# Setting the attention stage's constants at the start and loading its first two heads during the first stage of a fused transformer layer

## The reference

```python
xn  = layernorm(x)                                   # over the last axis
qkv = einsum('bld,ed->ble', xn, w_qkv); q, k, v = split(qkv, 3); q, k = rope(q), rope(k)
att = softmax(einsum('blhd,bmhd->bhlm', q, k) / sqrt(16))
a   = einsum('bhlm,bmhd->blhd', att, v) @ w_out.T
h   = silu(xn @ (w_gate/127).T) * (xn @ (w_up/127).T)    # integer weights
out = x + a + h @ (w_down/127).T
```

## Time and profile before

| | |
|---|---|
| median of 3 runs | 3239.01 us (3239.01 to 3239.97) |
| the profiled execution | 3237.97 us, its span 3236.2 us |
| mean granted TensorE clock | 0.972 of full speed |
| busy: PE, DVE, ACT, POOL | 92%, 87%, 75%, 13% of the span |
| stage A's last store issued | 544.21 us |
| first matmul of stage B | 576.85 us |

### The profile page before, as it was taken

The page is one execution under the profiler, slowest core; times in us unless marked ns, Lnnn a source line. Parts: engine busy times, 40 slices in busy tenths (PEclk is TensorE's granted clock), DMA queues, the critical chain, the costliest instruction groups (busy, mean ns, idle before and its releaser), DMA issues.

```text
span 3236.2 us, 65472 instructions
## 1 busy us (share of the span) xinstructions
PE 2986.2 (92%) x19736; PEld 915.1 (28%) x19736; DVE 2807.7 (87%) x3214; ACT 2413.1 (75%) x4609; POOL 435.8 (13%) x672
## 2 busy tenths in 40 slices
PE   5888886699999999999999999999999999999999
PEld 3555553122222222222222222222222222222225
DVE  6666764899999999999999999999999999999972
ACT  4445353288888888888888888888888888888883
POOL 2545445000000000000000000000000000000000
PEclk9999998699999999999999999999999999999999
DMA  2222222011111111111111011111111111111125
GB/s 92 78 96 76 88 84 63 26 28 29 29 28 29 28 29 28 29 28 29 28 29 30 27 31 27 32 26 31 28 30 28 30 28 30 28 30 28 30 61 163
DMA packets 124612, 137.04 MB, mean 42 GB/s; under 512 B 43264, under 2 KB 103296, under 8 KB 124288
## 3 DMA queue, kind: packets, MB, share of 16 engines
q1 hardware_dynamic: 124288, 132.79, 15.0%
HBM read 88.15 MB, written 34.08 MB: 38 GB/s over the span
## 4 chain that ended last, share of the span: by engine, by line
PE 77%; DVE 7%; issue 7%; POOL 3%; ACT 3%; DMA 1%; DVEq 0%; SPq 0%; ACTq 0%; POOLq 0%
PE psum L679 31%; PE psum L695 29%; PE psum L644 14%; DVE row_max L1196 2%; PE psum L627 2%; ACT probs L805 1%; POOL qk_rot L834 1%; POOL parts L840 1%; PE psum L554 1%; PE psum L577 1%; POOL hT L846 1%; ACT silu L749 1%; DVE xn L977 1%; DVE y_blk L1117 1%; DVE rot_s L1095 0%
## 5 line engine op out<-in xcount | busy, mean ns | idle before, releaser
L1196 DVE TENSOR_REDUCE row_max<-psum 128x1 f32<-128x1024 f32 x2048 | 2402.7, 1218 | 166.0 <-PE psum L644 142.9
L805 ACT ACTIVATE probs<-psum 128x512 f32<-128x512 f32 x4096 | 2130.6, 602 | 407.9 <-PE psum L695 405.0
L695 PE MATMUL psum<-q_op,k_op 51*128 51x512 f16 x4096 | 1249.7, 387 | 42.2 <-ACT probs L805 20.2
L644 PE MATMUL psum<-k_op,q_op 48*128 48x512 f16 x4096 | 1047.0, 393 | 97.1 <-issue 43.8
L679 PE MATMUL psum<-probs,v_op 128*32 128x512 f32 x8192 | 1104.6, 611 | 8.3
L695 PEld LDWEIGHTS psum<-q_op,k_op 51*128 51x128 f16 x4096 | 314.5, 94 | 1359.0 <-ACT probs L805 1235.3
L915 POOL TENSOR_TENSOR acc_sb<-acc_sb,inv_rows 128x512 f32<-128x512 f32 x64 | 81.6, 1276 | 1841.4 <-DMA inv_rows<-inv_dram 1841.4
L644 PEld LDWEIGHTS psum<-k_op,q_op 48*128 48x128 f16 x4096 | 217.5, 94 | 389.9 <-DVE row_max L1196 302.5
L679 PEld LDWEIGHTS psum<-probs,v_op 128*32 128x32 f32 x8192 | 163.3, 108 | 262.3 <-issue 244.1
L742 ACT ACTIVATE parts<-qk_rot 128x512 f16<-128x512 f32 x64 | 40.3, 630 | 244.1 <-POOL qk_rot L834 244.1
L554 PE MATMUL psum<-xnT,w 128*128 128x512 f16 x768 | 184.6, 388 | 9.9 <-DVE h L1108 9.9
(11 more groups left out here) (102 smaller groups left out, 1019.1 us busy)
## 6 DMA issues: line engine op xcount, KB each, us to landing
qk_dram<-staged SPq DMA_DIRECT2D x64, 256.0 KB, 2.9
q_op<-qk_dram SPq DMA_DIRECT2D x128, 128.0 KB
k_op<-qk_dram SPq DMA_DIRECT2D x128, 128.0 KB
x_ln<-in_x SPq DMA_DIRECT2D x16, 512.0 KB, 3.5
x_res<-in_x SPq DMA_DIRECT2D x16, 512.0 KB, 4.2
y_dram<-y_blk SPq DMA_DIRECT2D x16, 512.0 KB, 3.1
k_op<-qk_dram SPq DMA_DIRECT2D x128, 64.0 KB
q_op<-qk_dram SPq DMA_DIRECT2D x128, 64.0 KB
```

The lines of the kernel that those rows point to most:

```text
L644: mm = pe.matmul(bank(2 * half + j), q_op[r:r + ROWS, s, t * P:(t + 1) * P], k_op[r:r + ROWS, s, cols:cols + BANK], start=True, stop=True)
L695: pe.matmul(bank(b), k_op[r:e, h % SLOTS, t * P:(t + 1) * P], q_op[r:e, h % SLOTS, j * BANK:(j + 1) * BANK], start=True, stop=True).then_i ...
L805: nc.scalar.activation(probs[:, g2 % 2, j * BANK:(j + 1) * BANK], bank(b), ACT.Exp, scale=to_score).then_inc(s2_used, 1)
L1196: nc.vector.tensor_reduce(row_max[:, hl % 2, t, half:half + 1], psum[:, 2 * half * BANK:(2 * half + 2) * BANK], AX.X, ALU.max).then_inc(s1 ...
```

## The change

The eleven tensors get SBUF of their own (they are allocated with `keep`, before stage A's buffers, instead of over them). To make room `qk_rot` goes from four buffers to two, so `qk_sum(k, t)` now waits for `lo_part` of two tiles before instead of four. Six of the seven constants move to the start of GpSimd's list, around the cast of the down weights; the constant in `k_op` is written as pairs in 32-bit words. `inv_rows`, which still overlaps stage A's buffers, is cleared where it was, with a semaphore of its own (`rows_cleared`). `load_head(0)` and `load_head(1)`, 16 DMAs, move from after stage A to the point between SP's blocks 13 and 14; they wait for the stores of blocks 0 to 3, which hold the first sequence.

```diff
+STAB_ONE_PAIR = struct.unpack("<f", struct.pack("<ee", STAB_ONE, STAB_ONE))[0]
...
+    q_op = sb(keep, "q_op", [P, SLOTS, TILES * P], F16)
+    k_op = sb(keep, "k_op", [P, SLOTS, TILES * P], F16)
+    v_op = sb(keep, "v_op", [P, 2, TILES, 32])
...
-    qk_rot = sb(sa, "qk_rot", [P, BLK, 2 * D])
+    qk_rot = sb(sa, "qk_rot", [P, 2, 2 * D])
...
         with sp.Fori(1, NBLK - 2) as k:
             block_a(k, 2)
+        sp.wait_ge(b_const, 2)
+        sp.wait_ge(staged_out, 16 * N_STAGED * (TILES // BLK))
+        load_head(0, 0)
+        load_head(1, 0)
         block_a(NBLK - 2, 1)
         block_a(NBLK - 1, 0)
...
-        sp.wait_ge(b_const, 2)
-        load_head(0, 0)
-        load_head(1, 0)
-        sp.wait_ge(b_const, 7)
+        sp.wait_ge(rows_cleared, 1)
...
-        pe.wait_ge(b_const, 7)
+        pe.wait_ge(b_const, 6)
...
         nc.gpsimd.tensor_copy(identh[:, :], ident[:, :]).then_inc(identh_ready, 1)
+        k_words = k_op[:, :, :].rearrange("p s n -> p (s n)").bitcast(F32)
+        pool.wait_ge(identh_ready, 1)
+        nc.gpsimd.memset(k_words[32:HALF, :], STAB_ONE_PAIR).then_inc(b_const, 1)
+        pool.wait_ge(b_const, 1)
+        nc.gpsimd.memset(k_words[HALF + 32:P, :], STAB_ONE_PAIR).then_inc(b_const, 1)
         pool.wait_ge(wdown_loaded, 16)
+        pool.wait_ge(b_const, 2)
         nc.gpsimd.tensor_copy(nat["d"], nat["di"]).then_inc(down_float, 1)
+        pool.wait_ge(down_float, 1)
+        nc.gpsimd.memset(v_op[:, :, :, DH:32], 1.0).then_inc(b_const, 1)
+        ... (stab, zero and unit in the same way, each waiting for the one before)
+        pool.wait_ge(b_const, 6)
         pool.wait_ge(prep, MAT_MAX_READY)
...
-            if not (isinstance(k, int) and k == 0):
-                pool.wait_ge(parts_ready, BLK * (k - 1) + t + 1)
-            nc.gpsimd.tensor_tensor(qk_rot[:, t, :], rot_c[:, t % 2, :], rot_s[:, t % 2, :],
+            if t >= 2 or not (isinstance(k, int) and k == 0):
+                pool.wait_ge(parts_ready, BLK * k + t - 1)
+            nc.gpsimd.tensor_tensor(qk_rot[:, t % 2, :], rot_c[:, t % 2, :], rot_s[:, t % 2, :],
...
-        nc.gpsimd.memset(k_op[32:HALF, :, :], STAB_ONE).then_inc(b_const, 1)
-        ... (all seven constants)
+        nc.gpsimd.memset(inv_rows[:, :], 0.0).then_inc(rows_cleared, 1)
```

More of the change, by code:

```diff
@@ L14 @@
+import struct
 from contextlib import ExitStack
@@ L110, in layer_program @@
     exp_scale = sb(keep, "exp_scale", [P, 2])
+    q_op = sb(keep, "q_op", [P, SLOTS, TILES * P], F16)
+    k_op = sb(keep, "k_op", [P, SLOTS, TILES * P], F16)
+    v_op = sb(keep, "v_op", [P, 2, TILES, 32])
+    row_max = sb(keep, "row_max", [P, 2, TILES, 2])
+    neg_max = sb(keep, "neg_max", [P, TILES])
+    neg_rem = sb(keep, "neg_rem", [P, TILES])
+    neg_unit = sb(keep, "neg_unit", [P, TILES])
+    zero = sb(keep, "zero", [P, TILES])
+    unit = sb(keep, "unit", [P, TILES])
+    stab = sb(keep, "stab", [P, P // TILES, TILES], F16)
+    stabT = sb(keep, "stabT", [STAB_PARTS * TILES, P], F16)
     sa = ExitStack()
@@ L180, in layer_program @@
     sB = ExitStack()
-    q_op = sb(sB, "q_op", [P, SLOTS, TILES * P], F16)
-    k_op = sb(sB, "k_op", [P, SLOTS, TILES * P], F16)
     probs = sb(sB, "probs", [P, 2, TILES * P])
[L184 to L192, removed]
     acc_sb = sb(sB, "acc_sb", [P, 2, BANK])
@@ L258, in layer_program @@
     b_const = sem("b_const")
+    rows_cleared = sem("rows_cleared")
     qk_loaded = [sem(f"qk_loaded{s}") for s in range(SLOTS)]
@@ L385, in block_a @@
                 sp.dma_start(x_res[:, :, :], x_blocks[k + 1]).then_inc(xres_loaded, 16)
[L387 to L398, removed]
         def load_head(hl, i):
@@ L410, in load_head @@
                 sp.dma_start(k_op[r + DH:r + 3 * DH, s, :], src[1, 0:2]).then_inc(qk_loaded[s], 16)
+        sp.dma_start(x_res[:, :, :], x_blocks[0]).then_inc(xres_loaded, 16)
+        load_x(1)
+        block_a(0, 2)
+        with sp.Fori(1, NBLK - 2) as k:
+            block_a(k, 2)
+        sp.wait_ge(b_const, 2)
+        sp.wait_ge(staged_out, 16 * N_STAGED * (TILES // BLK))
+        load_head(0, 0)
+        load_head(1, 0)
+        block_a(NBLK - 2, 1)
+        block_a(NBLK - 1, 0)
+        sp.wait_ge(staged_out, 16 * N_STAGED * NBLK)
+        sp.wait_ge(y_out, 16 * NBLK)
+        sp.wait_ge(down_full, BLK * NBLK)
         def load_stab(hl, i):
@@ L741, in hi_part @@
                 act.wait_ge(partsT_full, BLK * k)
-            nc.scalar.activation(parts[:, t, 0, :], qk_rot[:, t, :], ACT.Copy).then_inc(part_hi, 1)
+            nc.scalar.activation(parts[:, t, 0, :], qk_rot[:, t % 2, :], ACT.Copy).then_inc(part_hi, 1)
         def block_a(k, last):
@@ L815, in _ @@
         nc.gpsimd.tensor_copy(identh[:, :], ident[:, :]).then_inc(identh_ready, 1)
+        k_words = k_op[:, :, :].rearrange("p s n -> p (s n)").bitcast(F32)
[3 more added lines that the diff above has]
+        nc.gpsimd.memset(k_words[HALF + 32:P, :], STAB_ONE_PAIR).then_inc(b_const, 1)
         pool.wait_ge(wdown_loaded, 16)
+        pool.wait_ge(b_const, 2)
         nc.gpsimd.tensor_copy(nat["d"], nat["di"]).then_inc(down_float, 1)
+        pool.wait_ge(down_float, 1)
+        nc.gpsimd.memset(v_op[:, :, :, DH:32], 1.0).then_inc(b_const, 1)
+        pool.wait_ge(b_const, 3)
+        nc.gpsimd.memset(stab[:, :, :], 0.0).then_inc(b_const, 1)
+        pool.wait_ge(b_const, 4)
+        nc.gpsimd.memset(zero[:, :], 0.0).then_inc(b_const, 1)
+        pool.wait_ge(b_const, 5)
+        nc.gpsimd.memset(unit[:, :], 1.0 / STAB_ONE).then_inc(b_const, 1)
+        pool.wait_ge(b_const, 6)
         pool.wait_ge(prep, MAT_MAX_READY)
@@ L839, in lo_part @@
             pool.wait_ge(part_hi, BLK * k + t + 1)
-            nc.gpsimd.tensor_tensor(parts[:, t, 1, :], qk_rot[:, t, :], parts[:, t, 0, :],
+            nc.gpsimd.tensor_tensor(parts[:, t, 1, :], qk_rot[:, t % 2, :], parts[:, t, 0, :],
                                     ALU.subtract).then_inc(parts_ready, 1)
@@ L1164, in _ @@
         block_a(NBLK - 1, 0)
-        dve.wait_ge(b_const, 7)
+        dve.wait_ge(b_const, 6)
         def add_y(half):
```

## The result

| | before | after |
|---|---|---|
| median | 3239.01 us | 3218.45 us (3216.76 to 3218.58, 4 runs) |
| ratio | | 0.9936, 95% interval 0.9919 to 0.9953 |
| profiled execution: own time, span | 3237.97, 3236.2 | 3218.38, 3216.6 |
| last store of stage A issued | 544.21 | 555.09 |
| first row maximum of stage B begins | 577.57 | 556.53 |

The change makes the kernel faster by 20.6 us, clearly more than 0.2%, but by less than the 27.0 us forecast, and 3218.45 lies outside the range of 3207 to 3217. The table says where to look: the gap between the stages went as forecast, but stage A ends 10.9 us later instead of 4.7, and stage B takes 1.5 us more. In stage A three things add up: it starts late, its blocks are longer by the new waits, and TensorE's clock falls to half in more of its blocks.

What follows compares the result with a forecast made beforehand. Bound: the chain from stage A's last store through fills and loads to stage B's first matmul, with TensorE, VectorE and ScalarE idle. −31.65 + 3.5 + 1.2 = −27.0 us, span 3209.2, median 3212.0 us, range 3207 to 3217.

Steps and rivals of the forecast that it cites:

- the growth of stage A: Stage A was to end 4.7 us later, from added GpSimd waits (3.5) and small fills at the start (1.2).
- The gap: Between stages A and B: fills and loads no longer delay the first matmul, only the branch out of the If; −31.65 us.
- The sixteen loads: SP's loads of heads 0 and 1, issued between blocks 13 and 14 in about 10 us: no cost, upper bound 1.
- The waits on `qk_rot`'s two buffers: GpSimd in stage A's blocks: two added waits a block at 0.11 us each, over 16 blocks, +3.5 us.
- rival B: The added GpSimd waits are hidden by other branches of a block's chain, so 3.5 us stay: 3208.5 us; chance 0.08.
- The constants: GpSimd's preparation: large fills fit its wait for w_down, four small ones behind the cast delay the all-reduce, +1.2 us.
- the port: Preparation: a GpSimd fill may hold VectorE's small operations 3.3 us through a shared port; taken as 0, upper bound 1.5.
- the configuration's delay: Preparation: 5.6 us from GpSimd's all-reduce configuration instruction to the first all-reduce, starting only behind the small fills.
- rival A: TensorE enters stage B at full clock and keeps it through 36 us of thin work, 2.0 us gained: 3210.0; chance 0.25.
- Stage B: From stage B's first matmul on, everything was to keep its distance, so no change in its length.

Runs made afterwards that it cites:

- The wait alone: The kernel before with four buffers of qk_rot, but sum t waiting for low part t-2: 3247.83 us, ratio 1.0025.
- the new order: The changed kernel with GpSimd's sum 2 moved behind low part 1, so no instruction waits for the one just ahead: 3208.2 us, ratio 0.9903.
- the small fills alone: The changed kernel with only the two large k_op fills moved behind the first all-reduce, four small ones left behind the cast: 3216.85 us, ratio 0.9926.
- two fillers: Unread matmuls added in stage B's steps 11 to 18, on both repairs plus stage A's filler: 48 rows 3198.73 us, 128 rows 3199.97 us.
- the kernel with dead code: The changed kernel with 54 matmuls added at the end of TensorE's Else, which is never run: 3238.23 us, ratio 1.0000.
- both repairs: The changed kernel with GpSimd's sum 2 behind low part 1 and all six fills behind the first all-reduce: 3206.89 us, ratio 0.9904.

## Why the prediction was wrong

By its own steps, in spans, forecast 3209.2 and measured 3216.6. The 7.4 us missed are 3.7 in dips of the clock, 1.5 in stage B, 1.3 in the waits and 1.2 in the constants, less 0.3 in the gap. The step that failed most is the growth of stage A, put at 4.7 us and measured at 10.9. Its largest missing part, TensorE's clock there, was put at nothing without a reason; the constants' risk was named and priced at nothing; the waits were right in kind and too small. The median missed by 6.5 us only: the forecast put it 1.0 us above the profiled execution, and it is 0.1 above.

**The gap** (−31.65): right, −31.9, in mechanism and number. The row of L605 gave what was late next, the branch out of the `If`; without the `If` VectorE's pause shrank from 1.47 to 0.60 us.

**The sixteen loads** (0): right, with 8.3 us of cover left though the issues took 12.3 us and not 10. With the loads back the gap is 20 us and block 14 no shorter.

**The waits on `qk_rot`'s two buffers** (+3.5): right in mechanism, too small. The price was read from small fills (0.06 us after the one ahead) and not from these 128x512 operations (0.14 us): 0.18 us a wait, of which 0.30 us a block show, 4.8 in all. The wait alone and the new order both show it; rival B, that they are hidden, is out.

**The constants** (+1.2, and 0 for the port): here the reasoning failed. The 1.2 us are real (1.14 with the small fills alone), but in the changed kernel what counted was the risk I priced at nothing: VectorE's first `tensor_scalar` held for 3.3 us, then `xn` took 1.5 more beside the cast. I had seen the first hold and let it hide exactly behind the configuration's delay, and left the second as an upper bound. The cost was 2.4 us. The row that I cited (1.24 us for an `xn` beside GpSimd) said that it could happen; a hold foreseen at two places belongs in the sum. The Trainium skill's rule (SBUF — State Buffer, Who interferes with whom) is a lock for a whole instruction, and the trace agrees: held to 10.13 us, where the fill ends at 10.11.

**TensorE's clock in stage A**: absent from the forecast. The stage grew by 8.4 us beside its late start of 2.4; the waits are 16 × 0.30 = 4.8 of it, and the other 3.7 are about what three more dips come to (4.1 by the lengths of the blocks that have them). The prediction did look at the clock, but only behind the gap; that the earlier trace rows hold no block with a dip is my choice of one block, and the two block lengths were in the trace. That the dips need the pause is shown: none with it filled, none at 1.7 us. That the added waits bring more of them is carried by the counts (6.6 against 3.7 on average) and by the wait alone, which costs 9.5 us where its blocks explain 4.8. Through what, the longer pause or the longer block, stays open.

**TensorE's clock in stage B** (rival A): wrong. In the changed kernel the clock fell within 1 us of the stage's first matmul (0.95 at 556 to 557 us, 0.50 from there on), though TensorE came at full speed and worked every 1.13 us, and the 2.0 us weren't gained. There a pause of 1.49 us stands just ahead of the stage; without the `If`, where that pause is 0.62, the clock held for 3.8 us of the thin work and fell all the same. So the thin work is enough. The Trainium skill's rule (TensorE: Matmul & The Clock Gate, HAM oscillation), by which gaps without matmuls lower the clock, fits stage A in kind; by gaps alone it would have kept the clock up here, and the trace differs. The measurement decides. What would raise it earlier stays open: two fillers didn't.

**Stage B** (0): 1.5 us longer, which is scatter as far as the runs show: ten profiles of kernels that leave it and TensorE's code ahead of it as they are have 2656.6 to 2660.5 us.

## What to carry to other kernels

A reuse of a buffer that makes an engine wait for the instruction just ahead costs little each time but can sit on the chain; putting one independent instruction in between bought back 0.37 us a block here for nothing. A fill moved into GpSimd's idle time can hold VectorE for all of its length, so look at what VectorE does there, not only at GpSimd's own row. And a comparison of two versions of a long looped kernel can be off by 20 us because code ahead of the loop has another length: read each stage's time from the profile before blaming the edit.

## What the runs showed of the hardware

At each jump back of stage B's loop VectorE waits 2.6 to 3.9 us for TensorE in the changed kernel, 14 times. Depending on where the body lies, a second stall of about 3 us ends some 5 us after the first: stage B took 2679.8 to 2684.4 us in the three kernels with it and 2654.3 to 2660.5 in the others, and 54 instructions that are never run were enough. That it is the next piece of code arriving late is argued, not shown: in the kernel with dead code the only DMA packet between 979 and 981 us, in the second stall, is one of instructions, and the changed kernel has none of instructions in that time. The row of the view of DMA queues, kernel with dead code, 979 to 981 us (queue, kind, packets, MB, share of the 16 DMA engines):

```profile
q8 instruction: 1, 0.02, 3.9%
```

The best version, both repairs and the fillers (of which those in stage B gained nothing that a run shows), takes 3198.73 us, 19.7 less than the change and 0.9875 (0.9858 to 0.9891) of the kernel before.
